# A software pipeline over token tiles one slot shorter: four V' products in one run, transpositions and scores of a tile in one slot

## The chip, the cores and the metric

The kernel runs on one NeuronCore of a Trainium2 chip. TensorE (PE) does the matrix products and the transpositions, VectorE (DVE), ScalarE (ACT) and GpSimd (POOL) do the elementwise work, SyncE (SP) issues the DMAs. The engines run side by side; each takes its own instructions strictly in order, and they meet in semaphores. The metric is the time of one execution on the device, in microseconds (us), lower is better; the time before is the median of 3 runs.

## The reference, cut to what matters

The input is 2048 tokens of 128 channels in fp32. A stack of six layers is run, then a retention block (left as it is by this change), then the same stack again. A layer is a windowed attention with 16 heads of 64 channels, followed by a gated feed-forward block (FFN):

```python
qkv = x @ Wqkv                         # 128 -> 3 * 1024, after a shift by one token of half the channels
q = l2norm(q) * qs;  k = l2norm(k) * ksc
q = q * cos * scale + rotate_half(q) * sin * scale      # k likewise, with 1 / scale
sim = q @ k.T * 8                      # windows of 32 queries see 64 keys
out = softmax(mask(sim)) @ v
x = out @ Wo + x
# FFN: layer norm, W1 to 2 * 341 channels, a * gelu(gate), W2 back to 128
x = ffn(shift(x)) + x
```

## The kernel before

Tokens go in tiles of 128 (16 tiles to a layer, 96 to a stack of six layers). The value projection and the output projection of each head pair are folded into one matrix M beforehand, so V' = x M already has 128 output channels per head, and P V' summed over the heads is the attention output. A stack is a software pipeline of slots, `LAST` of them: slot c works on tile c in one stage, on tile c-1 in the next, and so on (`live(c, lag, it)` says whether the tile with that lag exists). Each engine has a `slot` function in which its steps are written out by hand. Nothing is scheduled by a program: the order of the lines is the order on the engine.

The steps of PE in a slot, with the lag of the tile each works on: four products for q and k, called Q here (`project_qk`, L835, lag 0, banks QA[0] and QA[1] in turn); the transpositions of the rotated and normalised q and k (`qk_transpose`, L923, parts 0 to 3: parts 0, 1, 2 at lag 1 and part 3 at lag 2); the mask and the scores (`mask_scores` L933 and `scores` L949, lag 2, into both banks of VS); the transpositions of the softmax result P (`p_transpose`, L878, half 0 at lag 3 and half 1 at lag 4); the four V' products, one per 32 tokens (`project_v`, L899, lag 4, VS[0] and VS[1] in turn); the attention product P V' (`attend`, L854, lag 5, into TB[1]) and its transposition (`out_transpose`, L862, TB[1]). TB[0] is shared by parts 0 and 3 and by both halves of P; TB[1] by parts 1 and 2, the attention output and its transposition.

The FFN works on groups of four tiles. Its steps fall in four successive slots, and in the text a *period* is the time from one attention product to the next, named by the FFN work behind it: **centre** (L962, L967, lag 8 of the group's first tile), **up-0** (L977, L978), **up-1** (L977, L978, and the third part of the same product after the next Q product) and **down** (L986). In the first stack the matrices M of the next layer are computed as well (`fold_weights`, L1002, beside the centre step).

ACT squares each Q product (`square`, L452), copies the transposed tiles out of TB (`qk_out`, L466, and `p_out`, L478), does the softmax's exponential (L505), copies the attention output (L509), copies each V' product out of VS (`v_out`, L472) and does GELU (L486), for which it loads another table and loads the old one again (L486, L491, L530, L533). DVE rotates and sums squares (L602, L607, L615), finds the scores' maxima and subtracts them (L690, L694), sums P (L660) and adds the attention output to the residual (`attn_residual`, L634). POOL adds and normalises (L345, L352) and multiplies P by its reciprocal sum (L361).

What PE waits for at the steps that move: product 2 of V' waits for the copy of product 0 (`after(pe, s_ve, 4, m, w - 2, ...)`), product 3 for that of product 1, products 0 and 1 for DVE's last read of VS; part 1 of the transpositions waits for the residual addition, which reads TB[1] (`after(pe, s_res, 1, n - 5, ...)`); part 2 waits for the copy of part 1; the scores wait for the copy of part 3.

Of the kernel before, what the change touches and what calls it, by code (L numbers as in the profile page):

```python
# [8 lines left out]
DEPTH = 6  # L9
# [3 lines left out]
CH = INNER // P  # L13
# [11 lines left out]
LAST = TILES + 8  # L25
# [29 lines left out]
def build_macaron(nc, x, w_qk, w_vt, w_out, q_rows, w1, w2, prm_ffn, w_ret, gn, tables, consts, mask_n, ident,  # L55
# [5 lines left out]
    with ctx:  # L61
# [138 lines left out]
        def fold_piece(c, s):  # L200

            if s or c % 4 or not 4 <= c < 4 + 4 * CH // 2 * (DEPTH - 1):
                return None
            return (c - 4) // TPL + 1, (c - 4) // 4 % 4
# [6 lines left out]
        def _(sp):  # L211
# [42 lines left out]
            def slot(c, it, s):  # L254
# [26 lines left out]
                if (c - 11) % TPL == TPL - 4:  # L281
                    sp.wait_ge(s_dn, by_group(1, s * GROUPS + (c - 11) // 4, it, 1))
                    down_weights(nxt)
# [37 lines left out]
        def _(po):  # L321
# [8 lines left out]
            def slot(c, it, s):  # L330
# [25 lines left out]
                def softmax_mult():  # L356
                    m = n - 3
# [6 lines left out]
                def last_keys():  # L364
                    m = n - 2
# [22 lines left out]
                if live(c, 2, it) and (c - 2) % 4 == 3:  # L388
                    last_keys()
# [54 lines left out]
        def _(ac):  # L444
            def slot(c, it, s):
                n = s * TILES + c
                cen_g, up0_g, up1_g, up2_g = (group_of(c, first, it) for first in (8, 9, 10, 11))
# [20 lines left out]
                def v_out(w):  # L468
                    m = n - 4
# [30 lines left out]
                if live(c, 4, it):  # L500
                    p_out(4, 1)
                if live(c, 3, it):
                    m = n - 3
                    ac.wait_ge(s_z, by_tile(1, m, it, 1))
                    nc.scalar.activation(Z[:, m % 2, :], Z[:, m % 2, :], ACT.Exp, scale=8.0).then_inc(s_ex, 1)  # L505
                if live(c, 5, it):
                    m = n - 5
# [26 lines left out]
                if live(c, 1, it):  # L534
                    qk_out(1, 2)
# [6 lines left out]
                if live(c, 3, it):  # L542
                    p_out(3, 0)
                if (c - 7) % TPL == 0 and (it is not None or c < TILES):
                    l = (c - 7) // TPL
# [44 lines left out]
        def _(ve):  # L590
            def slot(c, it, s):
                n = s * TILES + c
                cen_g, up0_g, up1_g, up2_g = (group_of(c, first, it) for first in (8, 9, 10, 11))
# [37 lines left out]
                def attn_residual(rows, one):  # L631
                    m = n - 5
# [19 lines left out]
                if live(c, 5, it):  # L652
                    ve.wait_ge(s_ot, by_tile(1, n - 5, it, 1))
                    attn_residual(*HALVES[0])
                    attn_residual(*HALVES[1]).then_inc(s_res, 1)
                if live(c, 3, it):
                    m = n - 3
# [592 lines left out]
```

## Time and profile before

| | |
|---|---|
| median of 3 runs | 3482.67 us (3481.99 to 3487.38) |
| profiled execution | 3483.61 us, span 3481.8 us, mean granted clock 0.985 |
| PE | busy 3337.9 us, 96% of the span |
| DVE, ACT, POOL | busy 2858.4, 2433.7, 2342.3 us (82%, 70%, 67%) |
| DMA | 76.64 MB, mean 22 GB/s |

The page gives busy time by engine; "busy" of PE counts overlapping matmuls once. The end of a matmul is modelled and reaches over the start of the next, so a time on PE is read here from start to start of neighbouring rows. A wait that is shorter than this overlap doesn't show as idle time; it shows as a group that takes longer than the same group elsewhere.

### The profile page before, as it was taken

The page shows a single profiled execution, that of the slowest core. Times are in us where ns is not written, and L with a number is a line of the kernel's source. Part 1 is how long each engine was busy: PE and PEld are TensorE (multiplying, and loading weights), DVE is VectorE, ACT ScalarE, POOL GpSimd, SP SyncE. Part 2 cuts the span into 40 slices and gives each one's busy share as a digit, 9 for nine tenths or more (in the row PEclk, how much of TensorE's full clock was granted, in tenths as well). Part 3 has the DMA queues.
Part 4 walks back from the last instruction along what each step waited for, and adds up shares of the span by engine and source line. Part 5 has one row for each costly group of instructions (what it writes and reads, how often), then busy time and mean ns, then how long its engine had stood idle before and what let it go on. Part 6 is the DMA issues. An engine that isn't in the chain of part 4 may idle for free.

```text
span 3481.8 us, 123144 instructions
## 1 busy us (share of the span) xinstructions
PE 3337.9 (96%) x51660; PEld 1871.0 (54%) x51660; DVE 2858.4 (82%) x6052; ACT 2433.7 (70%) x4133; POOL 2342.3 (67%) x2188
## 2 busy tenths in 40 slices
PE   6999999999999999999788999999999999999996
PEld 3555555555555555555354555555555555555553
DVE  7888888888888888886468888888888888888883
ACT  3677777777777777777425777777777777777775
POOL 5777777777776777775137777777777777677771
PEclk8999999999999999999899999999999999999999
DMA  2001001001001001000100000000010000000000
GB/s 84 12 15 46 12 14 49 12 14 48 12 15 48 12 14 36 10 13 20 39 1 24 14 24 22 17 24 22 12 29 22 12 28 23 12 28 10 12 5 13
DMA packets 49223, 76.64 MB, mean 22 GB/s; under 512 B 7072, under 2 KB 37024, under 8 KB 47136
## 3 DMA queue, kind: packets, MB, share of 16 engines
q1 hardware_dynamic: 48672, 68.76, 6.3%
q8 instruction: 411, 6.73, 0.8%
q14 instruction: 140, 1.15, 0.1%
HBM read 61.39 MB, written 7.34 MB: 20 GB/s over the span
## 4 chain that ended last, share of the span: by engine, by line
PE 51%; POOL 22%; issue 15%; DVE 10%; ACT 1%; POOLq 0%; DMA 0%; SPq 0%; DVEq 0%; ACTq 0%
PE QA L835 10%; PE VS L899 10%; POOL QN L345 8%; POOL QN L352 8%; PE TB L923 6%; PE TB L854 5%; PE VS L949 4%; PE FB L986 4%; POOL Z L361 3%; PE TB L878 3%; DVE T L607 3%; DVE T L602 3%; PE FB L977 3%; PE FB L978 2%; POOL TAB L337 2%
## 5 line engine op out<-in xcount | busy, mean ns | idle before, releaser
L345 POOL TENSOR_TENSOR QN<-T 128x512 f32<-128x512 f32 x768 | 979.4, 1275 | 570.3 <-DVE T L607 551.7
L352 POOL TENSOR_TENSOR QN<-QN,RR 128x512 f32<-128x512 f32 x768 | 792.6, 1042 | 154.4 <-DVE RR L628 154.4
L835 PE MATMUL QA<-WQ,Y 128*128 128x512 f32 x1536 | 753.5, 603 | 23.0 <-DVE T L607 14.7
L899 PE MATMUL VS<-MW,Y 128*32 128x512 f32 x6144 | 738.5, 598 | 6.7 <-DVE Z L694 6.4
L602 DVE TENSOR_TENSOR T<-QA,TAB 128x512 f32<-128x512 f32 x768 | 525.4, 684 | 187.1 <-ACT SQ L452 178.2
L472 ACT ACTIVATE V<-VS 128x512 f32<-128x512 f32 x768 | 455.2, 601 | 251.4 <-PE VS L899 251.2
L923 PEld LDWEIGHTS TB<-CST,QN 128*128 128x128 f32 x3072 | 354.3, 141 | 491.8 <-issue 278.1
L452 ACT ACTIVATE SQ<-QA 128x512 f32<-128x512 f32 x768 | 441.4, 595 | 193.6 <-PE QA L835 182.2
L607 DVE TENSOR_TENSOR T<-QA,TAB 128x256 f32<-128x256 f32 x1536 | 572.4, 414 | 0.0
L361 POOL TENSOR_TENSOR Z<-Z,RC 128x512 f32<-128x512 f32 x384 | 394.4, 1048 | 237.2 <-DVE RC L664 235.1
L923 PE MATMUL TB<-CST,QN 128*128 128x128 f32 x3072 | 483.9, 280 | 34.4 <-DVE Y L634 20.9
L615 DVE TENSOR_REDUCE SSQ<-SQ 128x8 f32<-128x512 f32 x768 | 487.2, 675 | 0.0
L835 PEld LDWEIGHTS QA<-WQ,Y 128*128 128x128 f32 x1536 | 268.1, 193 | 245.9 <-issue 208.5
L854 PE MATMUL TB<-V,PT 128*32 128x128 f32 x12288 | 375.2, 274 | 0.0
L854 PEld LDWEIGHTS TB<-V,PT 128*32 128x32 f32 x12288 | 323.6, 110 | 33.4 <-issue 33.3
L466 ACT ACTIVATE KT<-TB 128x512 f32<-128x512 f32 x384 | 228.8, 596 | 140.5 <-PE TB L923 140.5
L899 PEld LDWEIGHTS VS<-MW,Y 128*32 128x32 f32 x6144 | 172.8, 109 | 282.3 <-issue 243.2
L949 PEld LDWEIGHTS VS<-KT,QT 64*32 64x32 f32 x24576 | 255.4, 105 | 96.5 <-issue 79.6
L949 PE MATMUL VS<-KT,QT 64*32 64x64 f32 x24576 | 289.0, 225 | 8.5 <-issue 8.1
L478 ACT ACTIVATE PT<-TB 128x512 f32<-128x512 f32 x384 | 228.1, 594 | 91.9 <-PE TB L878 91.8
L690 DVE TENSOR_REDUCE MX<-VS 128x8 f32<-128x512 f32 x384 | 246.1, 682 | 18.0 <-PE VS L949 17.6
L505 ACT ACTIVATE Z<-Z 128x1024 f32<-128x1024 f32 x192 | 203.9, 1062 | 66.9 <-DVE Z L694 65.9
(167 smaller groups left out, 4106.5 us busy)
## 6 DMA issues: line engine op xcount, KB each, us to landing
TAB<-in_tables SPq DMA_DIRECT2D x192, 128.0 KB, 2.1
WQ<-in_w_qk SPq DMA_DIRECT2D x48, 256.0 KB, 3.2
m_dram<-MW SPq DMA_DIRECT2D x6, 1024.0 KB, 5.6
MW<-m_dram SPq DMA_DIRECT2D x6, 1024.0 KB, 5.7
W1R<-in_w SPq DMA_DIRECT2D x12, 341.0 KB, 3.0
WS<-in_w_vt SPq DMA_DIRECT2D x6, 512.0 KB, 5.8
WS<-in_w_out SPq DMA_DIRECT2D x6, 512.0 KB, 5.3
W<-in_w SPq DMA_DIRECT2D x12, 192.0 KB, 2.9
```

What stands on the lines that cost most here:

```text
L345: po.tensor_tensor(QN[:, n % 2, k, :], T1[:, k, :], T2[:, k, :], ALU.add).then_inc(s_add, 1)
L352: po.tensor_tensor(heads(QN[:, m % 2, k, :]), heads(QN[:, m % 2, k, :]), RR[:, m % 2, 8 * k:8 * k + 8].unsqueeze(2).to_broadcast([P, 8, DH ...
L361: po.tensor_tensor(pv, pv, RC[:, m % 2, e, :].unsqueeze(1).unsqueeze(3) .to_broadcast([P, 2, CH, WIN]), ALU.mult).then_inc(s_pn, 1)
L472: nc.scalar.activation(V4[:, m % 4, w, :], VS[:, w % 2, :], ACT.Copy).then_inc(s_ve, 1)
L602: nc.vector.tensor_tensor(heads(T1[:, k, :]), heads(QA[:, b, :]), tab[:, 0:DHEAD].unsqueeze(1).to_broadcast([P, 8, DHEAD]), ALU.mult)
L607: ins = nc.vector.tensor_tensor(t2[:, :, half, :], q2[:, :, 1 - half, :], tab[:, DHEAD + 32 * half:DHEAD + 32 * half + 32].unsqueeze(1).to ...
L615: nc.vector.tensor_reduce(SSQ[:, n % 2, 8 * k:8 * k + 8], heads(SQ[:, k % 2, :]), AX.X, ALU.add)\
L835: mm(QA[:, k % 2, :], Y[:, j * P:(j + 1) * P], WQ[:, k, :], start=True, stop=True).then_inc(s_qk, 1)
L854: last = mm(TB[32 * w:32 * w + 32, 1, 0:P], PT[:, m % 2, b, 32 * w:32 * w + 32], v, start=(b == 0), stop=(b == CH - 1), tile_position=(0, ...
L899: last = mm(VS[32 * q:32 * q + 32, w % 2, :], Y[:, a:a + WIN], MW[:, l % 2, q, :], start=True, stop=True, tile_position=(0, 32 * q), skip_ ...
L923: last = nc.tensor.transpose(TB[:, (0, 1, 1, 0)[k], b * P:(b + 1) * P], QN[:, m % 2, k, b * P:(b + 1) * P], IDF)
L949: last = mm(bank[32 * w:32 * w + 32, :, ch, :], QT[r, m % 2, ch, w * WIN:(w + 1) * WIN], KT[r, ch, a:a + 2 * WIN].rearrange("p (a k) -> p ...
```

## The change

In every engine's `slot` the lags are shortened so that the pipeline has 103 slots per stack instead of 104, and the steps of a slot are put in another order.

```diff
-LAST = TILES + 8
+LAST = TILES + 7
...
-                cen_g, up0_g, up1_g, up2_g = (group_of(c, first, it) for first in (8, 9, 10, 11))
+                cen_g, up0_g, up1_g, up2_g = (group_of(c, first, it) for first in (7, 8, 9, 10))
... (ACT)
-                if live(c, 4, it):
-                    v_out(0)
-                    v_out(1)
+                if live(c, 3, it):
+                    for w in range(4):
+                        v_out(w)
                 if live(c, 1, it):
                     qk_out(1, 0)
-                if live(c, 4, it):
-                    v_out(2)
-                    v_out(3)
+                if live(c, 0, it):
+                    square(2)
                 if live(c, 1, it):
                     qk_out(1, 1)
-                if live(c, 0, it):
-                    square(2)
+                if live(c, 1, it):
+                    qk_out(1, 2)
+                if live(c, 0, it):
                     square(3)
-                if live(c, 2, it):
-                    qk_out(2, 3)
+                if live(c, 1, it):
+                    qk_out(1, 3)
...
-                if live(c, 1, it):
-                    qk_out(1, 2)
... (PE)
                     else:
-                        if edge:
-                            after(pe, s_pe, 2, n - 4, 1, it, s)
-                            after(pe, s_te3, 1, n - 3, 0, it, s)
-                        after(pe, s_te, 3, n - 1, 0, it, s)
+                        pe.wait_ge(s_te, by_tile(3, m, it, 1))
...
+                if live(c, 3, it):
+                    p_transpose(3, 1)
                 if live(c, 4, it):
-                    p_transpose(4, 1)
-                if live(c, 5, it):
                     attend()
-                if live(c, 4, it):
-                    project_v(0)
-                    project_v(1)
+                if live(c, 3, it):
+                    for w in range(4):
+                        project_v(w)
                 if live(c, 1, it):
                     qk_transpose(1, 0)
-                if live(c, 5, it):
+                if live(c, 4, it):
                     out_transpose()
                 if fold_piece(c, s):
                     fold_weights(*fold_piece(c, s))
-                if live(c, 4, it):
-                    project_v(2)
-                    project_v(3)
-                if live(c, 1, it):
-                    qk_transpose(1, 1)
                 if live(c, 0, it):
                     project_qk(2)
                 if up2_g is not None:
                     ffn_down(0)
+                if live(c, 1, it):
+                    qk_transpose(1, 1)
                 if live(c, 0, it):
                     project_qk(3)
+                if live(c, 1, it):
+                    qk_transpose(1, 2)
+                    qk_transpose(1, 3)
+                    mask_scores()
                 if up2_g is not None:
                     ffn_down(1)
                 if cen_g is not None:
                     ffn_centre()
                 if up2_g is not None:
                     ffn_down(2)
...
-                if live(c, 2, it):
-                    qk_transpose(2, 3)
-                    mask_scores()
-                if live(c, 1, it):
-                    qk_transpose(1, 2)
                 if up0_g is not None:
                     ffn_up(up0_g, 0)
                 if up1_g is not None:
                     ffn_up(up1_g, 1)
+                if live(c, 1, it):
+                    scores()
                 if live(c, 2, it):
-                    scores()
-                if live(c, 3, it):
-                    p_transpose(3, 0)
+                    p_transpose(2, 0)
```

The lags in DVE, POOL and SP are lowered by one in the same way (softmax, scores' maxima, residual, last keys, FFN), and `fold_piece` moves from slots with c % 4 = 0 to those with c % 4 = 3, so that it stays beside the centre step. The order of DVE's and POOL's own steps stays.

On PE, from the attention product of an up-0 slot to that of the next, before:

```order
L854 MATMUL TB<-V,PT 32x128 x32
L899 MATMUL VS<-MW,Y 32x512 x8
L923 MATMUL TB<-CST,QN 128x128 x4
L862 MATMUL TB<-CST,ON 128x128
L899 MATMUL VS<-MW,Y 32x512 x8
L923 MATMUL TB<-CST,QN 128x128 x4
L835 MATMUL QA<-WQ,Y 128x512 x2
L923 MATMUL TB<-CST,QN 128x128 x4
L933 MATMUL VS<-MASKN,IDB 128x512 x2
L923 MATMUL TB<-CST,QN 128x128 x4
L977 MATMUL FB<-XN,W 128x512
L978 MATMUL FB<-XN,W 128x512
```

and now (lines have moved up by two to five: L897 is V', L918 the transposition, L833 a Q product, L860 the transposition of the output):

```order
L852 MATMUL TB<-V,PT 32x128 x32
L897 MATMUL VS<-MW,Y 32x512 x16
L918 MATMUL TB<-CST,QN 128x128 x4
L860 MATMUL TB<-CST,ON 128x128
L833 MATMUL QA<-WQ,Y 128x512
L918 MATMUL TB<-CST,QN 128x128 x4
L833 MATMUL QA<-WQ,Y 128x512
L918 MATMUL TB<-CST,QN 128x128 x8
L928 MATMUL VS<-MASKN,IDB 128x512 x2
L973 MATMUL FB<-XN,W 128x512
L974 MATMUL FB<-XN,W 128x512
```

V' stands in one run directly behind P V', and the transpositions that stood behind its second half now stand between and behind the last two Q products.

On ACT, the copies and table loads of an up-1 slot up to the third GELU, before:

```order
L472 ACTIVATE V<-VS 128x512 x2
L466 ACTIVATE QT<-TB 128x512
L472 ACTIVATE V<-VS 128x512 x2
L466 ACTIVATE KT<-TB 128x4x128
L452 ACTIVATE SQ<-QA 128x512 x2
L466 ACTIVATE KT<-TB 128x4x128
L486 ACT_TABLE_LOAD
L486 ACTIVATE GE<-FB,PRB 128x512
L533 ACT_TABLE_LOAD
L466 ACTIVATE QT<-TB 128x512
L538 ACTIVATE LT<-NRM 128x32
L540 ACTIVATE RN<-LT,LNB 128x32
```

and now:

```order
L472 ACTIVATE V<-VS 128x512 x4
L466 ACTIVATE QT<-TB 128x512
L452 ACTIVATE SQ<-QA 128x512
L466 ACTIVATE KT<-TB 128x4x128
L466 ACTIVATE QT<-TB 128x512
L452 ACTIVATE SQ<-QA 128x512
L466 ACTIVATE KT<-TB 128x4x128
L486 ACT_TABLE_LOAD
L486 ACTIVATE GE<-FB,PRB 128x512
L533 ACT_TABLE_LOAD
L536 ACTIVATE LT<-NRM 128x32
L538 ACTIVATE RN<-LT,LNB 128x32
```

The copy of part 2 has moved from behind the second table load to before the first, and each square is now followed by a copy.

## Rows read from the trace of the kernel before

**Rows 1.** Busy time in a steady stretch (stretch, length, then each engine's busy time).
```profile
500.00:1000.00 500.00, 495.28 (x7982) 279.19 (x7984) 426.13 (x918) 371.62 (x628) 355.84 (x335) 1.00 0.08 25
```
**Rows 2.** Timeline of PE, an up-0 period (start us, length, then what).
```profile
1030.79 1.96 PE L854 MATMUL TB<-V,PT 128*32 128x128 f32 x64
1032.57 1.90 PE L899 MATMUL VS<-MW,Y 128*32 128x512 f32 x16
1034.40 0.66 PE L923 MATMUL TB<-CST,QN 128*128 128x128 f32 x4
1034.89 0.27 PE L862 MATMUL TB<-CST,ON 128*128 128x128 f32 x1
1035.09 1.92 PE L899 MATMUL VS<-MW,Y 128*32 128x512 f32 x16
1036.95 0.66 PE L923 MATMUL TB<-CST,QN 128*128 128x128 f32 x4
1037.44 1.88 PE L835 MATMUL QA<-WQ,Y 128*128 128x512 f32 x4
1039.16 0.60 PE L923 MATMUL TB<-CST,QN 128*128 128x128 f32 x4
1039.60 0.59 PE L933 MATMUL VS<-MASKN,IDB 128*128 128x512 bf16 x2
...
1044.18 1.88 PE L835 MATMUL QA<-WQ,Y 128*128 128x512 f32 x4
1046.08 0.63 PE L878 MATMUL TB<-CST,Z 128*128 128x128 f32 x4
1046.64 0.43 PE L854 MATMUL TB<-V,PT 128*32 128x128 f32 x8
```
**Rows 3.** Timeline of PE, an up-1 period, and where the next two begin.
```profile
979.91 1.96 PE L854 MATMUL TB<-V,PT 128*32 128x128 f32 x64
981.85 1.92 PE L899 MATMUL VS<-MW,Y 128*32 128x512 f32 x16
...
984.40 1.92 PE L899 MATMUL VS<-MW,Y 128*32 128x512 f32 x16
986.80 0.63 PE L923 MATMUL TB<-CST,QN 128*128 128x128 f32 x4 [0.48 <-DVE Y L634]
...
992.10 1.48 PE L949 MATMUL VS<-KT,QT 64*32 64x64 f32 x128
...
997.98 1.96 PE L854 MATMUL TB<-V,PT 128*32 128x128 f32 x64
...
1002.29 1.92 PE L899 MATMUL VS<-MW,Y 128*32 128x512 f32 x16
...
1014.51 1.96 PE L854 MATMUL TB<-V,PT 128*32 128x128 f32 x64
```
**Rows 4.** Timeline of ACT, the V' copies of the up-0 period.
```profile
1033.67 0.60 ACT L472 ACTIVATE V<-VS 128x512 f32<-128x512 f32 x1 [0.58 <-PE VS L899]
```
**Rows 5.** Timeline of PE, the last output transposition and what follows the residual.
```profile
3443.12 0.33 PE L862 MATMUL TB<-CST,ON 128*128 128x128 f32 x1 [0.40 <-ACT ON L509]
3444.13 1.13 PE L962 MATMUL FB<-Y,CST 128*128 128x512 f32 x2 [0.69 <-DVE Y L634]
```
**Rows 6.** Timeline of ACT, up-1 period into the down period.
```profile
992.21 0.69 ACT L486 ACTIVATE GE<-FB,PRB 128x512 f32<-128x512 f32 x1 [0.64 <-PE FB L978]
...
994.21 0.60 ACT L466 ACTIVATE QT<-TB 128x512 f32<-128x512 f32 x1
994.70 0.22 ACT L538 ACTIVATE LT<-NRM 128x32 f32<-128x32 f32 x1
...
997.78 1.28 ACT L491 ACT_TABLE_LOAD   x1
...
1001.62 1.11 ACT L472 ACTIVATE V<-VS 128x512 f32<-128x512 f32 x2
```
**Rows 7.** Busy time in a filling stretch (columns as in rows 1).
```profile
42.90:82.10 39.20, 28.00 (x338) 15.41 (x338) 34.87 (x72) 16.78 (x33) 32.52 (x32) 0.83 0.10 39
```

More of the change, by code:

```diff
@@ L200, in fold_piece @@
         def fold_piece(c, s):
-            if s or c % 4 or not 4 <= c < 4 + 4 * CH // 2 * (DEPTH - 1):
+            if s or c % 4 != 3 or c >= TPL * (DEPTH - 1):
                 return None
-            return (c - 4) // TPL + 1, (c - 4) // 4 % 4
+            return c // TPL + 1, c // 4 % 4
         def all_slots(engine, slot, s):
@@ L387, in slot @@
                     rot_add(2)
-                if live(c, 2, it) and (c - 2) % 4 == 3:
+                if live(c, 1, it) and (c - 1) % 4 == 3:
                     last_keys()
@@ L541, in slot @@
                         .then_inc(s_re, 1)
[L542 to L545, printed above, removed]
+                if live(c, 2, it):
+                    p_out(2, 0)
+                if (c - 6) % TPL == 0 and (it is not None or c < TILES):
+                    l = (c - 6) // TPL
                     ac.wait_ge(s_wf, by_layer(32, s * DEPTH + l, it, 32))
@@ L592, in slot @@
                 n = s * TILES + c
-                cen_g, up0_g, up1_g, up2_g = (group_of(c, first, it) for first in (8, 9, 10, 11))
+                cen_g, up0_g, up1_g, up2_g = (group_of(c, first, it) for first in (7, 8, 9, 10))
                 def rotate(k):
@@ L708, in slot @@
                     ins.then_inc(s_y, 1)
-                if (c - 7) % TPL == 0 and (it is not None or c < TILES):
-                    l = (c - 7) // TPL
+                if (c - 6) % TPL == 0 and (it is not None or c < TILES):
+                    l = (c - 6) // TPL
                     ve.wait_ge(s_y, by_group(1, s * GROUPS + l * NG, it, NG))
@@ L824, in slot @@
                 n = s * TILES + c
-                cen_g, up0_g, up1_g, up2_g = (group_of(c, first, it) for first in (8, 9, 10, 11))
+                cen_g, up0_g, up1_g, up2_g = (group_of(c, first, it) for first in (7, 8, 9, 10))
                 edge = c < AHEAD or c >= AHEAD + TILES - TPL
@@ L841, in attend @@
                     if edge:
-                        after(pe, s_res, 1, n - 6, 0, it, s)
+                        after(pe, s_res, 1, n - 5, 0, it, s)
                     after(pe, s_te, 3, n - 2, 2, it, s)
@@ L869, in p_transpose @@
                             after(pe, s_te, 3, n - 1, 0, it, s)
[L870 to L871 removed]
+                            after(pe, s_pe, 2, n - 3, 1, it, s)
+                        after(pe, s_te3, 1, n - 1, 0, it, s)
                     else:
                         if edge:
[L874 removed]
+                            after(pe, s_te3, 1, n - 2, 0, it, s)
                             after(pe, s_te, 3, n - 2, 0, it, s)
[L876 removed]
+                        after(pe, s_pe, 2, n - 3, 0, it, s)
                     for b in range(4):
@@ L892, in project_v @@
                         if edge:
-                            after(pe, s_ve, 4, n - 5, 2 + w, it, s)
-                        after(pe, s_z, 1, n - 3, 0, it, s)
+                            after(pe, s_ve, 4, n - 4, 2 + w, it, s)
+                        after(pe, s_z, 1, n - 2, 0, it, s)
                     else:
@@ L908, in qk_transpose @@
                             after(pe, s_te, 3, n - 2, 0, it, s)
-                            after(pe, s_te3, 1, n - 3, 0, it, s)
-                        after(pe, s_pe, 2, n - 4, 1, it, s)
+                            after(pe, s_te3, 1, n - 2, 0, it, s)
+                        after(pe, s_pe, 2, n - 3, 1, it, s)
                     elif k == 1:
@@ L913, in qk_transpose @@
                             after(pe, s_te, 3, n - 2, 2, it, s)
-                        after(pe, s_res, 1, n - 5, 0, it, s)
+                        after(pe, s_res, 1, n - 4, 0, it, s)
                     elif k == 2:
@@ L927, in mask_scores @@
                 def mask_scores():
-                    m = n - 2
+                    m = n - 1
                     if edge:
-                        after(pe, s_z, 1, n - 3, 0, it, s)
-                    after(pe, s_ve, 4, n - 4, 3, it, s)
+                        after(pe, s_z, 1, n - 2, 0, it, s)
+                    after(pe, s_ve, 4, n - 3, 3, it, s)
                     for e in range(2):
@@ L937, in scores @@
                 def scores():
-                    m = n - 2
+                    m = n - 1
                     j = m % 4
@@ L1052, in slot @@
                     ffn_down(2)
-                if (c - 7) % TPL == 0 and (it is not None or c < TILES):
+                if (c - 6) % TPL == 0 and (it is not None or c < TILES):
                     ffn_bias()
-                if live(c, 2, it):
-                    qk_transpose(2, 3)
-                    mask_scores()
-                if live(c, 1, it):
-                    qk_transpose(1, 2)
                 if up0_g is not None:
```

58 lines of the change are left out of this document (28 added, 30 removed).

## The prediction

> **What bounds the kernel now.** I read the busy times of a steady stretch first: PE is busy 495.28 of 500 us, DVE 426.13, ACT 371.62, POOL 355.84 [rows 1]. So PE sets the pace, and the change can give back only what PE loses between its products, or cost what it adds there. Next I read PE's timeline from start to start, for each of the four periods. They last 15.85 us (up-0, 1030.79 to 1046.64 [rows 2]), 18.07 (up-1, 979.91 to 997.98), 16.53 (down, 997.98 to 1014.51 [rows 3]) and 16.28 (centre, 1014.51 to 1030.79 [rows 2, 3]): 66.73 us per group of four tiles, and 24 groups in each of two stacks make 48. Last I looked at ACT and DVE beside the steps that move, for what PE would meet there.
>
> **Losses that the new order takes off PE.** Matmuls on a quarter of the columns of the array (P V' and V', "128*32" in the rows) alternate with whole-array ones ("128*128").
> 1. V'. The Q products are the yardstick: two of them take 1.72 us (1037.44 to 1039.16), 0.86 each. Two V' products have the same 512 columns each, and take 1.83 behind P V' and 1.86 behind a whole-array step [rows 2], together 3.69. One run of four is 2 x 1.72 plus one surcharge of 0.11, 3.55: 0.14 less.
> 2. The output's transposition takes 0.20 (1034.89 to 1035.09) when V' follows; one of four transpositions among whole-array steps takes 0.44 / 4 = 0.11 (1039.16 to 1039.60): 0.09 less, since a Q product follows it now.
> 3. Part 1 of the transpositions takes 0.49 behind V' (1036.95 to 1037.44) and 0.44 between Q products: 0.05 less (I count 0.02 in up-1 and down, where it starts after a wait and has part of this behind it).
>
> That is 0.28 in up-0, 0.25 in down and up-1. In the centre period of the first stack the fold stands behind the output's transposition, so only 0.19 goes there, and 0.28 in the second stack; 0.24 on average. The move of mask and scores changes no neighbour: the scores still follow one whole-array step, and P's transposition follows them.
>
> The Trainium skill, page TensorEngine Tiling (Array Packing), section Key Properties, says that a change of tiling mode, unlike a change of tile within one, drains TensorE. The differences of 0.11 to 0.14 us in rows 2 agree with it, and by it the change removes one entry and one exit per slot, which is the sum above.
>
> **Waits that go.** In up-1 the second half of V' lasts 2.40 us (984.40 to 986.80) against 1.86, and the row names DVE's residual: 0.54 of wait [rows 3]. The residual must read TB[1] before part 1 is written. In the new order a Q product (0.86) stands between the output's transposition and part 1, and DVE was late there because of its own queue (rotations, sums), so the whole 0.54 goes. In up-0 the second half of P's transposition starts 1.90 behind the Q pair instead of 1.72, and P V' follows it 0.56 later: 0.18 of wait in front, some 0.03 behind, 0.21. It waits for ACT to empty TB[0]; on ACT the copy of part 2 no longer stands in front (0.49, from 994.21 to 994.70 [rows 6], the same in up-0). But that copy, and part 3's, now come before the first table load. From the start of part 2 on PE, ACT can start copying after 0.64 (0.44 and 0.20 until a copy begins), then 0.48 + 0.48 + 0.60 for copy, square, copy (a copy lasts 0.60, and the next starts 0.12 before its end): 2.20, and the load (1.28) ends at 3.48; PE begins the scores at 0.44 + 0.44 + 0.43 + 0.86 + 0.95 = 3.12. GELU stands at 3.50, 0.38 behind the scores' start, where it stood at 0.11 (992.21 against 992.10). So ACT gains 0.49 - 0.27 = 0.22, just enough for the 0.21. In up-1 the first V' product begins 1.94 after P V' starts, against 1.78 in up-0: DVE's read of the scores ends late. It hangs on the same ACT steps and moves with PE by the same amount, so I leave these 0.17.
>
> **Waits that come.**
> - Third and fourth V' product. ACT starts the first copy 1.10 us after the run starts (1033.67 against 1032.57 [rows 2, 4]), it takes 0.60, and PE resumes 0.07 after the end of such a copy (in the down period, 1001.62 + 0.60 = 1002.22 against 1002.29 [rows 3, 6]): 1.77, when PE wants it at 1.72. 0.05 of wait, some 0.06 with the weights' load laid bare; the fourth product is then late by the same and just meets its own copy. Bounds: 0, as the weights may be loaded ahead, to 0.15. I take 0.06 for up-0, up-1 and centre.
> - The same in **down** is the costly one. ACT comes there from a GELU with two table loads. The last load ends at 999.06, 1.08 after P V' starts, and the first V' copy ends at 1002.22, 3.16 behind the load. Before, PE wanted the third product at 1002.29 only. Now it wants it 1.77 + 1.72 = 3.49 after P V' starts. With the 0.22 that ACT gained in up-1 (its last GELU then just meets PE), the load ends at 0.86, the copy at 4.02, PE resumes at 4.09: 0.60 of wait. The 0.07 that PE lost there before goes. Bounds 0.3 (ACT gains the whole 0.49) to 0.82 (it gains none).
> - Part 1 behind the residual. The output's transposition now comes 1.8 us later, so DVE, early in up-0 and in the centre period of the second stack, waits for it. At the end of the second stack, where DVE is idle, a PE step that needs the residual starts 1.01 after that transposition (3443.12 to 3444.13 [rows 5]), against 0.11 + 0.86 = 0.97 here. 0.04 of wait, I take 0.05, and none where a fold or a down product stands between. Bounds 0 to 0.15.
> - Part 2 behind the copy of part 1, both in TB[1]: square 2 ends 0.1 before the copy may start, and the copy ends about as the next Q product does: 0.02. Bounds 0 to 0.15, the square's whole lateness.
>
> DVE's softmax sum slips behind the later residual by about 1.1 us; DVE is idle 15% of the stretch [rows 1] and waits there for the third square, so it hides; uncovered it would cost up to those 1.1 us per period, which rival C's kind of slowness would bring. The last keys, now copied one slot earlier for a tile whose part 3 also comes one slot earlier, stand as before.
>
> **The sum.** Up-0: -0.28 - 0.21 + 0.06 + 0.05 + 0.02 = -0.36. Up-1: -0.25 - 0.54 + 0.06 + 0.02 = -0.71. Down: -0.25 - 0.07 + 0.60 + 0.01 = +0.29. Centre: -0.24 + 0.06 + 0.03 + 0.02 = -0.13. Together -0.91 per group, times 48 = -44 us. One slot less at each stack's end: the work stays, the idle of one slot goes. PE idles 11.2 us in about four filling slots [rows 7], 2.8 each; 0 to 2.8 per stack, I take 2, so -4. The profiled execution took 3483.61 us: 3483.61 - 48 = 3435.6, and as it stands 0.9 us over the median, **3435 us**, 1.4% faster. Its own range, from the bounds of the four waits: 3410 to 3460.
>
> **The rivals.**
> - *No new waits at all* (B). PE would save everything: 0.49 + 0.96 + 0.32 + 0.24 = 2.01 per group, -96 - 4, 3383 us. For it: ACT is busy only 74% of the stretch. Against: the down period's queue of ACT is bound by its loads, not by its share.
> - *ACT sets V'* (C, slower). Every run of four V' products waits like the one in down, because ACT still has the exponential or the output's copy before the first V' copy. Price 0.60 instead of 0.06 in three periods: +1.62 - 0.91 = +0.71 per group, +34 - 4, 3513 us. It decides from the point where ACT is over 0.5 us later at V' than now; now it has waited 0.58 us when the product is ready [rows 4], which is what speaks against.
>  The Trainium skill has this as a rule (same page, section PSUM Bottleneck): tiling speeds up TensorE but not the emptying of PSUM, which may become the bottleneck. The trace agrees only in the down period.
> - *The surcharge isn't in the switch* (D). If the 0.09 to 0.14 belong to the loads of weights or to other neighbours and stay, while the waits are as I say: -0.91 + 1.02 = +0.11 per group, +5 - 4, 3484 us.
> - *Small waits larger* (E). Copies alternate with squares on ACT now, and parts 1 and 2 share a bank. At all the upper bounds (V' 0.15 in three periods, down 0.82, part 1 0.15 where it waits, part 2 0.15 everywhere) they add 0.27 + 0.22 + 0.2 + 0.5 = 1.2, so +0.3 per group, +14 - 4, 3493 us; halfway there, 3464 us.
>
> **How the numbers follow.** Forecast 0.60, B 0.12, C 0.07, D 0.07, E 0.14. A measurement tells about 0.2%, 7 us, from no change. Faster by more: the forecast, B and E up to two thirds of its way, 0.81. Within: D and a little of E, 0.09. Slower: C and the rest of E, 0.10. The range 3395 to 3486 leaves out C and most of B.
>
> **What would show it.** In PE's timeline: one run of 32 V' rows lasting 3.6 us (right) in up-0 and about 4.15 in down; over 4 in up-0 is C. The output's transposition 0.11 to the Q product; if 0.20, D. No "Y L634" wait of 0.5 in up-1. P's second half 1.72 behind the Q pair. Periods near 15.5, 17.35, 16.8 and 16.15. I am wrong if the down wait spreads into the other periods, or if DVE, now waiting for the later residual, delays the scores' maxima and so the first V' product.

## The result, and the profile after

The kernel after takes **3534.69 us** (median; 3531.58 to 3545.39, 4 runs), the kernel before 3482.84 beside it (3481.99 to 3487.38): ratio 1.0154, 95% interval 1.0142 to 1.0167. It is 51.9 us slower, where 3435 us was forecast and 3395 to 3486 was the range.

Head of the page of after: span, busy time of each engine, and the queue that brings the instructions (packets, MB, share).
```profile
span 3535.2 us, 123261 instructions
PE 3337.5 (94%) x51660; PEld 1833.2 (52%) x51660; DVE 3003.5 (85%) x6052; ACT 2435.3 (69%) x4133; POOL 2335.5 (66%) x2188
q8 instruction: 411, 6.73, 0.8%
```
A steady stretch of after, columns as in [rows 1]:
```profile
500.00:1000.00 500.00, 491.36 (x7827) 269.78 (x7820) 443.07 (x912) 366.27 (x624) 352.99 (x333) 1.00 0.08 25
```
In 500 us PE gets through 7827 products, not 7982, and is busy 491.4 us, not 495.3. That is 1.9% fewer, where the whole run lost 1.5% (the two stretches don't begin at the same piece of work). The clock granted is 1.00 in both.

PE's timeline of after, one group of four tiles with nothing unusual in it (start us, length, what, and in brackets the idle before and who ended it). It answers to [rows 2, 3]:
```profile
956.70 1.96 PE L852 MATMUL TB<-V,PT 128*32 128x128 f32 x64
...
973.21 1.96 PE L852 MATMUL TB<-V,PT 128*32 128x128 f32 x64
974.98 3.68 PE L897 MATMUL VS<-MW,Y 128*32 128x512 f32 x32
978.59 0.66 PE L918 MATMUL TB<-CST,QN 128*128 128x128 f32 x4
979.08 0.27 PE L860 MATMUL TB<-CST,ON 128*128 128x128 f32 x1
979.19 1.02 PE L833 MATMUL QA<-WQ,Y 128*128 128x512 f32 x2
980.13 0.63 PE L918 MATMUL TB<-CST,QN 128*128 128x128 f32 x4
980.60 1.02 PE L833 MATMUL QA<-WQ,Y 128*128 128x512 f32 x2
981.54 1.07 PE L918 MATMUL TB<-CST,QN 128*128 128x128 f32 x8
...
986.59 1.88 PE L833 MATMUL QA<-WQ,Y 128*128 128x512 f32 x4
988.30 0.63 PE L876 MATMUL TB<-CST,Z 128*128 128x128 f32 x4
988.86 1.96 PE L852 MATMUL TB<-V,PT 128*32 128x128 f32 x64
...
1006.40 1.95 PE L852 MATMUL TB<-V,PT 128*32 128x128 f32 x64
1008.17 1.90 PE L897 MATMUL VS<-MW,Y 128*32 128x512 f32 x16
1010.54 1.92 PE L897 MATMUL VS<-MW,Y 128*32 128x512 f32 x16 [0.47 <-ACT V L472]
1012.39 0.66 PE L918 MATMUL TB<-CST,QN 128*128 128x128 f32 x4
...
1023.39 1.95 PE L852 MATMUL TB<-V,PT 128*32 128x128 f32 x64
```
From start to start: centre 16.51 us, up-0 15.65, up-1 17.54, down 16.99. Together 66.69, against 66.73 before. So where nothing unusual happens the new order is as fast as the old one. The whole trace says the same: the medians of these periods are 15.65, 17.54, 16.99 and 16.50, and only the centre period of the second stack is another one, 15.72 against 15.64 before. The V' run lasts 3.61 (978.59 - 974.98), the output's transposition 0.11 up to the Q product, the run in down 4.22, and no row names the residual: these are the marks that the prediction set for itself.

The unusual is in the waits of PE. Waits that no engine's semaphore ended, before and then after, there with the largest other wait (what waited, us in total, times, longest):
```profile
PE VS L949 <- issue: 8.1, 12, 1.9
PE TB L1119 <- issue: 1.2, 1, 1.2
PE QA L835 <- issue: 0.5, 1, 0.5
PE TB L878 <- issue: 0.4, 2, 0.2
```
```profile
PE VS L945 <- issue: 48.1, 30, 2.4
PE VS L897 <- ACT V L472: 20.0, 44, 0.6
PE TB L876 <- issue: 10.2, 7, 1.8
PE FB L963 <- issue: 4.4, 3, 1.7
PE QA L833 <- issue: 2.5, 4, 0.8
PE TB L1111 <- issue: 1.2, 1, 1.2
```
"Issue" is time in which PE waited for nothing that the profile shows. It sums to 10.2 us before and to 66.4 after: **56 us more**, where the two profiled spans differ by 53.4 (3535.2 - 3481.8). All else on PE together is thus 3 us shorter than before. Of the 66.4, 48.1 stand inside the scores, which hold no wait between their first product and their last. One of these, on PE, and on PE's loads of weights (PEld) in the same place:
```profile
1052.99 1.42 PE L945 MATMUL VS<-KT,QT 64*32 64x64 f32 x120
1055.92 0.32 PE L945 MATMUL VS<-KT,QT 64*32 64x64 f32 x8 [1.52 <-issue]
```
```profile
1053.40 0.85 PEld L945 LDWEIGHTS VS<-KT,QT 64*32 64x32 f32 x79
1055.93 0.15 PEld L945 LDWEIGHTS VS<-KT,QT 64*32 64x32 f32 x7 [1.68 <-issue]
```
Loads and products stop together, 8 products before the end. In this slot the queue "instruction" moved one packet of 16,384 bytes, asked for at 1053.27, 2.65 us before PE went on. I then counted, over the whole trace, PE's loads, products and semaphore instructions. Their number, 105,359, over 411 packets is 256 per packet. All 32 gaps above 0.25 us inside the scores of after (53.5 us) stand at number 194 or 195 modulo 256 (the mark, below), as do all 16 (11.1 us) before, and each of after's ends 2.2 to 2.9 us behind the request for a packet. So I read it that PE has run out of instructions there; experiments 4 and 5 test it.

A tile's scores are 128 loads and 128 products, 256 instructions in 1.41 us: one mark falls into each of the 192 runs of scores. Sorted by how many instructions of the scores stand ahead of it (the us hold the normal step of 0.06 of each gap; the last two columns say how long behind the mark before this one a packet was asked for, median, before and after):

| mark at | gaps before | gaps after | request, before | request, after |
|---|---|---|---|---|
| 0 to 127 | 0 of 95, 0 us | 0 of 95, 0 us | 0.3 us | 0.3 us |
| 128 to 191 | 1 of 44, 0.3 us | 5 of 48, 8.3 us | 0.0 us | 0.5 us |
| 192 to 223 | 3 of 24, 2.6 us | 8 of 22, 14.0 us | 2.1 us | 3.3 us |
| 224 to 255 | 12 of 29, 9.1 us | 19 of 27, 33.0 us | -0.1 us | 2.5 us |

A mark late in the scores has the one before it shortly ahead of them, most often on the transpositions (L918; in the last line 4.9 us lie between the two, against some 11 us in the first). The gaps end as if the packet asked for behind the first mark were needed at the second, and it is asked for later in the kernel after.

### The profile page after: what moved, and what is told of

Same layout as the page of the kernel before. It is cut to its first block, busy times and chain, and to the rows that moved or that the text cites. A ratio compares the mean times of both kernels' runs of the same rounds, so it can differ in the third digit from the quotient of the medians.

```text
span 3535.2 us, 123261 instructions
## 1 busy us (share of the span) xinstructions
PE 3337.5 (94%) x51660; PEld 1833.2 (52%) x51660; DVE 3003.5 (85%) x6052; ACT 2435.3 (69%) x4133; POOL 2335.5 (66%) x2188
## 4 chain that ended last, share of the span: by engine, by line
PE 72%; ACT 11%; issue 9%; POOL 5%; DVE 2%; DMA 0%; SPq 0%; POOLq 0%; ACTq 0%; DVEq 0%
PE VS L897 16%; PE QA L833 15%; PE TB L918 10%; PE TB L852 7%; PE VS L945 6%; PE TB L876 4%; PE FB L982 4%; ACT L486 3%; ACT SQ L452 2%; POOL QN L345 2%; PE FB L973 2%; PE VS L928 2%; POOL QN L352 2%; PE FB L974 2%; ACT GE L486 2%
## 5 line engine op out<-in xcount | busy, mean ns | idle before, releaser
L833 PE MATMUL QA<-WQ,Y 128*128 128x512 f32 x1536 | 784.7, 609 | 22.1 <-DVE T L605 11.9
L897 PE MATMUL VS<-MW,Y 128*32 128x512 f32 x6144 | 714.2, 596 | 26.7 <-ACT V L472 20.0
L918 PEld LDWEIGHTS TB<-CST,QN 128*128 128x128 f32 x3072 | 333.8, 141 | 431.5 <-issue 353.4
L918 PE MATMUL TB<-CST,QN 128*128 128x128 f32 x3072 | 451.9, 280 | 6.5 <-ACT KT L466 2.7
L897 PEld LDWEIGHTS VS<-MW,Y 128*32 128x32 f32 x6144 | 158.4, 109 | 434.1 <-ACT V L472 291.7
L945 PE MATMUL VS<-KT,QT 64*32 64x64 f32 x24576 | 291.9, 225 | 58.2 <-issue 48.1
L466 ACT ACTIVATE QT<-TB 128x512 f32<-128x512 f32 x384 | 229.3, 597 | 160.5 <-PE TB L918 160.5
L833 PEld LDWEIGHTS QA<-WQ,Y 128*128 128x128 f32 x1536 | 254.9, 194 | 156.8 <-issue 128.7
L632 DVE TENSOR_TENSOR Y<-TB,Y 64x128 f32<-64x128 f32 x384 | 111.3, 290 | 205.0 <-PE TB L860 198.6
L876 PE MATMUL TB<-CST,Z 128*128 128x128 f32 x1536 | 245.5, 282 | 15.2 <-issue 10.2
```

Source lines behind the costliest of these rows:

```text
L833: mm(QA[:, k % 2, :], Y[:, j * P:(j + 1) * P], WQ[:, k, :], start=True, stop=True).then_inc(s_qk, 1)
L897: last = mm(VS[32 * q:32 * q + 32, w % 2, :], Y[:, a:a + WIN], MW[:, l % 2, q, :], start=True, stop=True, tile_position=(0, 32 * q), skip_ ...
L918: last = nc.tensor.transpose(TB[:, (0, 1, 1, 0)[k], b * P:(b + 1) * P], QN[:, m % 2, k, b * P:(b + 1) * P], IDF)
L945: last = mm(bank[32 * w:32 * w + 32, :, ch, :], QT[r, m % 2, ch, w * WIN:(w + 1) * WIN], KT[r, ch, a:a + 2 * WIN].rearrange("p (a k) -> p ...
```

## The experiments

All times are medians of runs beside the kernel before on the same chip, and ratios are to that; there it took 3483.2 us (first set), 3483.7 (second), 3483.3 (third) and 3485.1 (last).

**1. Does the place in the packets matter?** Short products ahead of the first tile shift all that follows by 32, 64 or 96 instructions.
```
+            for _ in range(16):        # 8, 16, 24 (32, 64, 96 instructions)
+                mm(FB[:, 1, 511:512], IDF, CST[:, 1, 0:1], start=True, stop=True)
```


> The changed kernel with 8 one-column matmuls (two loads and two matmuls each, 32 PE instructions) put in front of PE's program, which shift every later PE instruction by 32 places and do nothing else; they cost under 2 us. The trace of the changed kernel shows 27 waits inside the score products of the steady stretches, 47 us together, all at the same place counted in PE instructions (194 modulo 256), and each ends 2.2 to 2.9 us after a 16 KB packet of instructions was requested. Theory F (PE runs out of instructions): shifting the program moves the waits, up-0 slots leave the window in which they occur (scores starting at 197 to 223 modulo 256), the waits inside scores fall below 20 us and the time to 3490, give or take 15. Rival R (the waits belong to data, semaphores or memory traffic at this place of the schedule): nothing moves, 3535 to 3540 and 47 us as before.

> As a_pad32 with 16 such matmuls, 64 places. Theory F: up-0 slots are out of the window, the slots that come into it are down slots, where more time lies between the fetch and the scores: waits inside scores below 25 us, time 3480 to 3505. Rival R: 3535 to 3540.

> As a_pad32 with 24 such matmuls, 96 places. Theory F: every second up-1 slot comes into the window (scores starting near 200), so the waits there are as many as those that go from up-0: 30 to 50 us of waits, time 3515 to 3540, above a_pad32 and a_pad64. Rival R: 3535 to 3540, the same as the other two.

> The kernel before with the same 64 places of shift. It has 11 waits inside scores, 10 us in all. Theory F: the shift changes these and nothing else, the time moves by -10 to +40 us, in step with the sum of its waits inside scores. Rival R: 3483 to 3486, and the same 10 us of waits.

Measured: after shifted by 32, 64 and 96: 3551.66, 3544.94, 3537.47 us (ratios 1.0174 [1.0138, 1.0210], 1.0172 [1.0152, 1.0192], 1.0163 [1.0132, 1.0193]); before shifted by 64: 3482.53 (1.0001 [0.9991, 1.0010]). The gaps stay at 194 or 195 modulo 256, though the code under these numbers is now other code. That ties them to the count of instructions. But no shift gains anything: 32, 31 and 33 gaps instead of 32. The slots' lengths in instructions aren't multiples of 256, so every part of a slot meets the mark in time, whatever the start. Hoping for a lucky shift was wrong: with the first shift 3490 us and under 20 us of gaps were expected, with the second 3480 to 3505 and under 25, and the "issue" waits in the scores are 56.9, 51.0 and 42.6 us where after has 48.1. By its times alone the rival (3535 to 3540 whatever the shift) was nearer; only the places of the gaps speak against it. In the shifted kernel before these waits are 4.3 us instead of 8.1. The times of the three also don't follow the waits one for one: the third has 12 us less "issue" in all than after (54.2 against 66.4) and takes no less time.

**2. Which part of the change?** First the V' run and the move of part 1 alone, with all lags as before:
```
 PE:  project_v(0) project_v(1) +project_v(2) +project_v(3)  qk_transpose(1, 0)  out_transpose  fold
      -project_v(2) -project_v(3) -qk_transpose(1, 1)  project_qk(2)  ffn_down(0)  +qk_transpose(1, 1)
 ACT: v_out(0..3) in one run, qk_out(1, 0), square(2), qk_out(1, 1), square(3)
```


> The kernel before with one part of the change: the four V' products in one run behind P V', and part 1 of the transpositions behind the third Q product; lags, part 2, part 3 and the scores stay as they were. Theory T (the new place of parts 2 and 3, mask and scores is what makes PE run out of instructions inside the scores): the waits inside scores stay near the 11 us of the kernel before, the four periods give -0.17 (up-0), -0.73 (up-1), +0.50 (down), -0.15 (centre), -0.55 per group, 3457 us. Theory V (the run of V' brings these waits): they are near 50 us and the time is 3490 to 3510.

Measured: 3479.16 us, 0.9988 [0.9978, 0.9998]. The "issue" waits in its scores are 11.0 us, against 8.1 before and 48.1 after, so the run doesn't bring them. But the time misses the 3457 that was expected by 22 us: the run costs in down slots, 0.58 us in each of 44:
```profile
PE VS L897 <- ACT V L472: 25.6, 44, 0.7
PE VS L947 <- issue: 11.0, 16, 2.0
```
Then the kernel after with V' in two and two again, in every slot (first text) and in down slots only (second), and after with part 3, mask and part 2 back directly ahead of the up products (third):
```
+                first = 2 if up2_g is not None else 4     # down slots only; 2 in every slot
+                    for w in range(first): project_v(w)
+                    for w in range(first, 4): project_v(w)   # behind the fold
```


> The changed kernel with V' split again: two products, part 0, the output's transposition, the fold, two products; all else as changed. In both theories it loses the waits of the third and fourth product (about 0.6 us in 48 down periods and 0.05 in the others, 37 us) and of part 1 (8 us), and gives up 0.23 us in each of 192 slots (44 us), so about even but for the waits inside scores. Theory T: they stay near 50 us, 3525 to 3540. Theory V: they fall to 10 to 20 us, 3490 to 3500.

> The changed kernel with V' split only in the down slots, where ACT comes late from GELU and its table loads. The run of V' there takes 4.22 us by the trace of the changed kernel, of which 0.6 is wait; split it should take 1.83 + 1.86. All theories: -0.6 + 0.23 = -0.37 us in 48 periods, -18 us against the changed kernel, 3517; the waits inside scores stay near 50 us in theory T, and fall by a quarter at most in theory V.

> The changed kernel with part 3, mask and part 2 (in this order, of the tile of lag 1) moved back to where such steps stood before, behind the down and centre products and directly ahead of the up products and the scores. ACT copies part 3, then part 2, behind the fourth square. Theory T: the waits inside scores fall from 53 to 10 to 20 us; PE then waits 0.6 to 1.0 us for the last copy in front of the scores in down and centre slots (96 periods, about +70 us), so 3530 to 3580. Theory V: waits inside scores stay near 50 us, and the time is 3590 to 3620.

Measured: 3529.73 (1.0142 [1.0120, 1.0163]), 3518.95 (1.0107 [1.0092, 1.0123]) and 3548.93 (1.0197 [1.0182, 1.0212]). The down wait is thus worth 16 us. V' split in every slot gains 4 or 5, which is within the noise, and leaves 37.1 us of "issue" in the scores, less than the 50 that were expected if the run has no part in them and far more than the 10 to 20 if it brings them. The third was to show that the new place of the parts is what starves PE: its waits in the scores were to fall to 10 to 20 us. They fall to 35.4 only, so the place isn't the main cause. And the move back is a loss of its own:
```profile
PE VS L944 <- ACT QT L466: 70.0, 102, 0.7
PE VS L944 <- issue: 35.4, 34, 2.2
```
With the short lag and the old order the scores stand directly behind part 2, and wait 0.7 us for ACT's copy of it in about every second slot. So putting the parts early, as the change does, is right if the lag is shortened.

**3. The lag alone, and the run without the lag.**
```
 a_lag = after, V' two and two, part 3 / mask / part 2 directly ahead of the up products
 b_vd  = before, V' run of four except in down slots, part 1 behind the third Q product
```


> The kernel after with V' split 2+2 in every slot and part 3, mask and part 2 back directly ahead of the up products; what is left of the change is the distance (part 3, mask and scores one slot after the projections, and not two) and part 1 behind the third Q product. Theory 'the distance costs': 3544 us, if the two single variants add up (3530 and 3549 against 3535 for the kernel after), 25 or fewer gaps in the scores. Rival 'it is the dense order of parts 1, 2 and 3 that costs': close to the kernel before, 3480 to 3495 us, and about 10 gaps.

> The kernel before with four V' products in one run in three of four slots, split 2+2 as before in the down slots, and part 1 of the transpositions behind the third Q product (behind it and the first down product in down slots). Theory 'the run is good where ACT is free; the shortened distance between a tile's transpositions and its scores is what costs': the kernel with the run everywhere took 3479 us with 44 waits of 1.17 us in the down slots (-56 us without them), the switch surcharge comes back there (48 x 0.25 = +12): 3435 us. Rival 'the run brings nothing in the other slots either': 3475 to 3483 us, and the waits show again somewhere else in the row. In-score gaps: about 10, as before, by both.

Measured: 3545.41 us (1.0177 [1.0161, 1.0192]) and **3460.96 us** (0.9933 [0.9918, 0.9948]). The lag costs, the rest gains 22 us. But "the distance costs" hides two things in the first: 70.1 us of waits for the copy of part 2, as above, and 30.8 us of "issue" in the scores, in 29 gaps where 25 or fewer were expected. The agreement of 3545 with the 3544 that I had expected is therefore no proof that a short lag must starve PE. The second missed its 3435 by 26, and the price it started from is where that lies: it took the waits in the down slots of the kernel with the run everywhere for 56 us (1.17 each), and the row above has 25.6 (0.58 each). Measured, splitting the down slots brought 19 us (3479 to 3461) and not 44. Its periods (medians) are 15.73 (up-0), 17.43 (up-1), 16.57 (down) and 16.60 in the centre period of the first stack, which was 16.28 before: there the run costs, too.

**4. Fewer instructions.** Both kernels without 28 of each tile's 64 score products. Each is two loads and two products in the trace, so the scores shrink from 256 instructions to 144 (the expectations below count only half of them: it is 112 fewer here, and 106 fewer in the next pair, not 50):
```
-                        for e in range(2):
+                        for e in range(1 if ch < CH - 1 else 2):
```


> The kernel after, which leaves out 28 of the 64 score products of each tile (the second head of each pair, but for the last pair). Theory 'PE runs out of instructions': a tile's scores are 72 and not 128 instructions long, so that the gaps inside the scores fall to under a third (below 18 us in all), and the difference to the kernel before with the same products left out falls from 51 to 10 to 30 us. Rival 'the difference is waits for other engines': the gaps may fall, but the difference stays at 45 us or more, or grows, since PE reaches the waits sooner. In both kernels up to 192 x 0.62 = 119 us of PE's work goes.

> The kernel before with the same 28 of the 64 score products of each tile left out: 3365 us if PE sets the pace throughout (3484 - 119), up to 3430 if ACT and DVE take part of it back. It is the base for the kernel after with the same products left out.

Measured: after 3431.68 us, before 3447.70 (ratios to the whole kernel before 0.9848 [0.9832, 0.9864] and 0.9897 [0.9882, 0.9912]). **The sign turns**: with these products left out the change gains 16 us. No gap above 0.25 us is left in the scores of either, nor behind them: all that remains of "issue" is one wait of 1.2 us in each. The mark can't stand behind instruction 143 of the scores now, and it never made a gap ahead of 128. Both times miss what was expected of products that last 0.62 us per tile (before: 3365 to 3430 us): the scores still take 1.04 us, as the rows of the next pair show, so that only 0.37 per tile or 71 us were left out. But PE also has less to do, which could cover a loss; hence the last pair.

**5. Fewer instructions, no less work in time.** The same products left out, and three long mask products ahead of the scores:
```
+                    for e in (0, 1, 0):
+                        mm(VS[:, e, :]..., IDB[:, :], MASKN..., start=False, stop=False)
```


> The kernel after with 28 of the 64 score products of each tile left out, and three more whole-array mask products (0.216 us each, 0.65 us) put directly ahead of the scores: PE is as busy as in the kernel after, with 50 instructions fewer per tile. Theory 'PE runs out of instructions': the change stays a gain here; this kernel takes 5 to 35 us less than the kernel before with the same edit, as with the products left out alone (3432 against 3448 us), and has less than 5 us of gaps in the scores. Rival 'the products left out only gave PE slack in which the loss hid': with the slack filled again this kernel is 40 to 60 us slower than the kernel before with the same edit.

> The kernel before with 28 of the 64 score products of each tile left out and three mask products of 0.216 us put directly ahead of the scores. PE is as busy as in the kernel before: 3475 to 3490 us by both theories, less the 11 us of gaps that the kernel before has in its scores.

Measured: after **3497.98** us (1.0041 [1.0026, 1.0055]), before **3503.13** (1.0052 [1.0035, 1.0069]): the change gains 5 us, the low end of what was expected. The base missed its 3475 to 3490, since PE has more to do than with all products: the three products take 0.74 us in a row and not 0.65, and the scores 1.04 us, 1.78 together against 1.41. Here in after of this pair:
```profile
1008.46 0.81 PE L940 MATMUL VS<-MASKN,IDB 128*128 128x512 bf16 x3
1009.20 1.11 PE L949 MATMUL VS<-KT,QT 64*32 64x64 f32 x72
1010.24 0.66 PE L876 MATMUL TB<-CST,Z 128*128 128x128 f32 x4
```
Head and instruction queue of after and of before in this pair, with the only "issue" wait of each:
```profile
PE 3369.0 (96%) x41484; PEld 1806.8 (52%) x41484; DVE 2998.4 (86%) x6052; ACT 2434.8 (70%) x4133; POOL 2332.7 (67%) x2188
q8 instruction: 332, 5.44, 0.7%
PE TB L1115 <- issue: 1.2, 1, 1.2
```
```profile
PE 3373.4 (96%) x41484; PEld 1848.1 (53%) x41484; DVE 2858.3 (82%) x6052; ACT 2431.3 (69%) x4133; POOL 2341.7 (67%) x2188
q8 instruction: 331, 5.42, 0.6%
PE TB L1123 <- issue: 1.2, 1, 1.2
```
PE is busy 3369 us in the first, more than in the kernel after (3337.5), so slack isn't what hid the loss. From +51.9 to -5.2 is a swing of 57 us, and the "issue" waits that are gone in one and not in the other are the 56 of above. This also shows that DVE's busy time, 3003 against 2859 us with the same 6052 instructions, isn't the cause: it is as high here (2998), and the loss is gone. (Most of it lies in two small steps, which from before to after go from 527 to 1016 ns, L621, and from 200 to 590 ns, L677; why wasn't looked into.)

**6. The change only where it pays.** Before, with the run of four and part 1 moved only in slots that have neither a down product nor a piece of the fold, lags as before:
```
+                run = up2_g is None and not fold_piece(c, s)
+                    for w in range(4 if run else 2): project_v(w)
+                if live(c, 1, it) and run:
+                    qk_transpose(1, 1)                       # behind the third Q product
```


> The kernel before, changed only where the change pays: V' in one run of four and part 1 behind the third Q product in the slots that have neither a down product nor a piece of the fold; all else as before. The variant with the run in three of four slots took 3461 us; its slots with a fold lasted 16.67 us against 16.28 before (24 of them: -9 us), its down slots 16.60 against 16.54 (48: -3 us). Theory 'each slot's loss is its own': 3449 us. Rival 'the neighbours take it back' (ACT and DVE set the pace over several slots): 3458 to 3465 us.

Measured: **3452.37 us** (3444.26 to 3456.90), 0.9905 [0.9890, 0.9920], near the 3449 that was expected if each slot's loss is its own, and the fastest of those that leave nothing out. Its centre period in the first stack and its down period are back at 16.28 and 16.53. Its "issue" wait in the scores, and a steady stretch, in which PE gets through 8145 products (before: 7936 in the same stretch):
```profile
PE VS L953 <- issue: 6.8, 11, 2.3
```
```profile
1000.00:1500.00 500.00, 499.11 (x8145) 279.11 (x8143) 443.09 (x932) 373.42 (x638) 360.51 (x339) 1.00 0.08 24
```

## Why the prediction was wrong

It was off by 99.7 us, and two things make up 98 of it.

**The missing term, 56 us.** The prediction had no term for PE's own supply of instructions. None of its rivals had it either; all of them asked which engine PE would wait for. The case it names as wrong (the down wait spreading, DVE delaying V') didn't happen. [Rows 2] had the ground for it: the scores are 128 loads and 128 products in 1.41 us, a whole packet, and a line of the waits before already read "issue: 8.1, 12, 1.9". That line was small, and so it wasn't asked what its size depends on. Experiments 4 and 5 show that it is the number of instructions in the scores; experiment 2, that the V' run isn't what mainly raises it: before with the run has 11.0 us of it, after without the run 37.1 (24 times). What the variants with the loss have in common is the short lag, by which parts 1, 2, 3 and the scores of a tile stand in one slot, each part behind a copy of ACT. Over the whole trace a packet is asked for 0.9 us (median) behind a mark, and 2.8 us where that mark is on the transpositions (26 cases; 0.2 us before, 30 cases). A likely reason is that the waits in front of the parts hold back the request as they hold back PE. That is not shown: no run took the waits out and left the count. So it is shown that the added 56 us are PE's own supply, most of them inside the scores; why it comes later after the change stays open.

**Small waits, 42 us.** In clean periods of the first stack the change was to bring -0.91 us per group, and brings -0.04 (66.69 - 66.73); 0.87 x 48 = 42. The whole trace agrees: without the "issue" waits the span is 3 us shorter than before, where 48 were forecast. The 4 us for the shorter ends of the stacks are within these 3 and can't be told apart. By the prediction's own terms, in us per group:

| term | forecast | measured, after | missed by |
|---|---|---|---|
| V' run in up-0, up-1, centre | 3.61 | 3.61 to 3.64 | 0 to 0.03 |
| V' run in down | 4.15 | 4.22 | 0.07 |
| output's transposition to Q | 0.11 | 0.11 | 0 |
| Q ahead of part 1 | 0.91, 0.86 in up-1 and centre | 0.94 (979.19 to 980.13), 0.96 behind the fold | 0.03, 0.08, 0.10 |
| part 1 | 0.44 | 0.47 (0.44 in centre, down) | 0.03 twice |
| Q ahead of part 2 | 0.88 | 0.94; 0.99 in centre | 0.06 three times, 0.11 |
| scores behind the centre product | 0.95, no wait | 1.05 | 0.10 |

The centre period shows the last three (after; it answers to no row of before, since the parts stood elsewhere), and below it ACT in the same stretch:
```profile
1030.12 1.12 PE L833 MATMUL QA<-WQ,Y 128*128 128x512 f32 x2
1031.08 0.60 PE L918 MATMUL TB<-CST,QN 128*128 128x128 f32 x4
1031.52 1.02 PE L833 MATMUL QA<-WQ,Y 128*128 128x512 f32 x2
1032.51 1.06 PE L918 MATMUL TB<-CST,QN 128*128 128x128 f32 x8
1033.41 0.59 PE L928 MATMUL VS<-MASKN,IDB 128*128 128x512 bf16 x2
1033.84 1.02 PE L958 MATMUL FB<-Y,CST 128*128 128x512 f32 x2
1034.89 1.47 PE L945 MATMUL VS<-KT,QT 64*32 64x64 f32 x128
```
```profile
1031.28 0.60 ACT L452 ACTIVATE SQ<-QA 128x512 f32<-128x512 f32 x1 [1.21 <-PE QA L833]
1031.77 0.59 ACT L466 ACTIVATE KT<-TB 128x512 f32<-128x512 f32 x1
...
1034.14 0.60 ACT L466 ACTIVATE KT<-TB 128x512 f32<-128x512 f32 x1
```
Part 1 ends at about 1031.52, but the square of the third Q product holds ACT until 1031.77, and the copy ends at 1032.36: part 2 starts at 1032.51 and not at 1032.38. The forecast had 0.02 here with 0.15 as its bound, and the rows have 0.08 (0.94 - 0.86) to 0.13 (0.99 - 0.86). In the same way the scores, 1034.89, meet the end of part 3's copy (1034.14 + 0.60 = 1034.74). I had followed part 3's copy only in up-0 and had called the centre's neighbours unchanged.

Point by point. Right: the surcharge is in the switch (the run of four at 3.61, the transposition at 0.11), so rival D fell; the residual's wait goes in up-1 (no row names it; the period is 17.54, forecast 17.36, before 18.07); the P half's wait goes in up-0 (986.59 to 988.30 is 1.71); the down slots pay for ACT (a run of 4.22 us, 4.15 forecast), and splitting there brought 16 us back. Rival C fell: only down waits. Rival E was the right one in kind for the second thing: the small waits together ate the gain. Take the added "issue" waits off, and 3534.7 - 56 = 3479 is left, between E's halfway point (3464) and all its upper bounds (3493). But E named only a part of it: part 1 at 0.47 instead of 0.44, the wait ahead of part 1 in up-1 and centre and the one ahead of the scores in the centre stand in none of its bounds. The range that the sum gave for itself, 3410 to 3460, was also narrower than its own four bounds, which add up to some 3405 to 3493. Wrong: the step "waits that come" undersized everywhere, and the whole list of what PE can wait for.

## What to carry to other kernels

Where one engine is busy 99% of the time, ask also what feeds that engine: a run of many short instructions (here 256 in 1.4 us) lives on a packet asked for before it, and with steps that wait moved to just ahead of it the request came later. An "issue" line in the waits, inside a run that holds no wait, is the sign, however small it is; what its size depends on is the question to ask. Moving independent work closer to its consumer removes a stage, but each "0.02 us" wait it adds comes in every period. And an edit that pays in some kinds of slots and not in others can be made only there: here that, with the lags left as they were, gave a gain of 33 us in place of a loss of 52.

## What the runs showed of the hardware

- PE's instructions come in packets of 16,384 bytes, one per 256 of its loads, products and semaphore instructions (105,359 and 411; with products left out 85,007 and 332). In after a packet took 0.9 to 1.7 us (median 1.0), and PE went on 2.2 to 2.9 us behind the request.
- In the dense runs of short products PE stood up to 2.7 us without an instruction, always at the same number modulo 256 (194 or 195); shifting the program by 32 to 96 instructions moves the code under the mark and not the mark.
- Leaving 28 of 64 score products out shortened a tile's scores from 1.41 to 1.04 us, 71 us in all, and brought before only 36. The up-0 period is 15.84 us either way, so it is not set by PE's work alone, although PE is 99% busy in [rows 1].
